# Causal attention: GpSimd zeroes the diagonal block's future probabilities in place of a triangle matmul on the scores

## The reference, cut to what matters

```python
scores = jnp.einsum('bqhd,bkhd->bhqk', q, k) * hd ** (-0.5)
causal = jnp.tril(jnp.ones((S, S), bool))
scores = jnp.where(causal, scores, jnp.finfo(scores.dtype).min)
attn = jax.nn.softmax(scores, axis=-1)
o = jnp.einsum('bhqk,bkhd->bqhd', attn, v).reshape(B, S, D)
```

## Time and profile before

| | |
|---|---|
| median of 3 runs | 2627.32 us (2627.03 to 2632.26) |
| the profiled execution | 2615.49 us, of which 2613.7 us from the first to the last instruction |
| busy over the span | TensorE 81%, VectorE 58%, ScalarE 41%, GpSimd 11% |
| mean granted clock of TensorE | 0.90 |
| causal attention | about 903 to 1385 us of the span |

### The profile page before, as it was taken

The page is one execution under the profiler, slowest core; times in us unless marked ns, Lnnn a source line. Parts: engine busy times, 40 slices in busy tenths (PEclk is TensorE's granted clock), DMA queues, the critical chain, the costliest instruction groups (busy, mean ns, idle before and its releaser), DMA issues. The chain is left out here.

```text
span 2613.7 us, 46760 instructions
## 1 busy us (share of the span) xinstructions
PE 2105.6 (81%) x14586; PEld 1292.0 (49%) x14587; DVE 1521.3 (58%) x3119; ACT 1076.9 (41%) x1974; POOL 294.3 (11%) x348
## 2 busy tenths in 40 slices
PE   7748999999599549999995850199999964899987
PEld 4402333333355325555554640188888852555654
DVE  5746777776166436666653864344444435677763
ACT  3415666666122115555551112233333323465552
POOL 1000000000111000000000006500000013312100
PEclk9968999999699769999997765599999987999999
DMA  6742333320357534444414538411111132111100
GB/s 204 261 122 70 85 97 86 93 74 22 117 161 241 178 112 112 118 131 120 130 61 148 174 110 286 156 49 45 49 49 48 45 100 65 53 61 41 56 9 17
DMA packets 212155, 271.53 MB, mean 104 GB/s; under 512 B 24929, under 2 KB 161018, under 8 KB 212018
## 3 DMA queue, kind: packets, MB, share of 16 engines
q1 hardware_dynamic: 205250, 252.70, 31.8%
q0 software_dynamic: 6144, 16.79, 1.9%
q10 hardware_dynamic: 624, 0.30, 0.1%
HBM read 159.77 MB, written 108.86 MB: 103 GB/s over the span
## 5 line engine op out<-in xcount | busy, mean ns | idle before, releaser
L749 ACT ACTIVATE a_prob<-a_psE 128x512 f32<-128x512 f32 (+3 forms) x1024 | 500.3, 519 | 508.5 <-PE a_psE L646 254.5
L630 PE MATMUL a_psS<-a_K,a_Q 97*128 97x512 bf16 (+3 forms) x1024 | 360.9, 358 | 117.7 <-DMA a_Q<-a_nrow 45.5
L782 DVE TENSOR_REDUCE a_nm<-a_psS 128x2 f32<-128x1024 f32 x256 | 312.9, 1225 | 136.6 <-PE a_psS L630 135.6
L643 PE MATMUL a_psE<-a_Q,a_K 100*128 100x512 bf16 (+3 forms) x1024 | 356.8, 351 | 37.9 <-DMA a_Q<-a_nrow 26.4
L779 DVE TENSOR_REDUCE a_nm<-a_psS 128x1 f32<-128x128 f32 (+3 forms) x512 | 238.3, 487 | 175.8 <-PE a_psS L633 173.6
L643 PEld LDWEIGHTS a_psE<-a_Q,a_K 100*128 100x128 bf16 x1024 | 103.2, 101 | 274.0 <-ACT a_prob L749 192.4
L1407 PE MATMUL ex_psH<-ex_xT,ex_w1h 128*128 128x256 f16 x1872 | 232.7, 275 | 3.6 <-ACT ex_xT L1366 2.1
L656 PE MATMUL a_psO<-a_prob,a_V 128*32 128x512 f32 (+3 forms) x2048 | 233.7, 529 | 1.4 <-ACT a_prob L749 1.4
L1421 PE MATMUL ex_psY<-ex_w2h,ex_hl 128*128 x1872 | 229.4, 272 | 0.5 <-DVEq L1332 0.4
L1375 ACT ACTIVATE ex_hf<-ex_psH,ex_b 128x256 f32<-128x256 f32 x312 | 131.2, 472 | 233.8 <-PE ex_psH L1407 233.8
L630 PEld LDWEIGHTS a_psS<-a_K,a_Q 97*128 97x128 bf16 x1024 | 103.5, 102 | 242.7 <-DVE a_nm L779 74.3
(11 more groups left out here) (253 smaller groups left out, 3154.6 us busy)
## 6 DMA issues: line engine op xcount, KB each, us to landing
s_qk<-t_parts SPq DMA_DIRECT2D x64, 384.0 KB, 3.2
s_v<-t_vaug SPq DMA_DIRECT2D x16, 1024.0 KB, 6.5
a_V<-s_v SPq DMA_DIRECT2D x64, 256.0 KB
s_o<-a_on SPq DMA_DIRECT2D x64, 256.0 KB, 2.1
t_cin<-s_o SPq DMA_DIRECT2D x16, 1024.0 KB, 8.4
ex_stage<-in_w SPq DMA_DIRECT2D x16, 1024.0 KB, 6.7
a_K<-s_qk SPq DMA_DIRECT2D x64, 192.0 KB
a_Q<-s_qk SPq DMA_DIRECT2D x64, 192.0 KB
```

The costliest lines, as they stand in the source:

```text
L630: last = pe.matmul(bank[:, 0:n], Q6[s][0:K_MAX, h, t * P:(t + 1) * P], K6[s][0:K_MAX, h, 0:n], start=True, stop=not causal)
L643: last = pe.matmul(bank[:, 0:S - q0], K6[s][0:K_EXP, h, t * P:(t + 1) * P], Q6[s][0:K_EXP, h, q0:S], start=True, stop=not causal)
L749: act.activation(prob[j % NP_BUF][:, 0:n], psE[j % NE][:, 0:n], ACT.Exp).then_inc(p_ready, 1)
L782: dve.tensor_reduce(nm[s % NM_BUF][:, t - 1:t + 1, h], psS_all[:, (j - 1) % NS:j % NS + 1, :], axis=AX.X, op=ALU.max, negate=True).then_in ...
```

## The change

The triangle `cmk` and its matmul in `shifted` go away. The exponential is then taken of unmasked scores on the diagonal block too. Behind each exponential GpSimd overwrites the future places of the first 128 columns of the `prob` tile by 0, with a select on position (`affine_select`), in place. `weigh` waits for the new semaphore `masked` in place of `p_ready`. The triangle `cmq` for the maxima stays. In the phase `a0` `masked` is `p_ready` itself and nothing changes.

GpSimd's loop now has 16 selects a step, and `rcx` of group G - 1 stands between the selects of units 10 and 11.

```diff
-    cmk = c.sb("cmk", [P, P], BF16)
+    masked, seen = (c.sem("masked"), c.sem("seen")) if causal else (p_ready, None)
...
+            def widen(n, s):
+                pool.wait_ge(rc_ready, n)
+                pool.tensor_tensor(rcx[s][:].rearrange("p (h m) -> p h m", m=HP),
+                                   rc[s][:].unsqueeze(2).to_broadcast([P, TT * GH, HP]),
+                                   one[:].to_broadcast([P, TT * GH, HP]), ALU.mult).then_inc(rcx_ready, 1)
+
+            def future_out(G, j):
+
+                pool.wait_ge(p_ready, G * U + j + 1)
+                pool.sem_inc(seen, 1)
+                square = prob[j % NP_BUF][:, 0:P]
+                pool.affine_select(out=square, in_=square, compare_op=ALU.is_ge, fill=0.0, base=0,
+                                   pattern=[[1, P]], channel_multiplier=-1).then_inc(masked, 1)
+
+            def step(G, s):
+                for j in range(U):
+                    future_out(G, j)
+                    if j == 10 and not (isinstance(G, int) and G == 0):
+                        widen(G, (s - 1) % 2)
+
+            if causal:
+                steps(pool, step)
+                widen(G_ALL, (G_ALL - 1) % 2)
+                return
...
-                last = pe.matmul(bank[:, 0:S - q0], K6[s][0:K_EXP, h, t * P:(t + 1) * P], Q6[s][0:K_EXP, h, q0:S],
-                                 start=True, stop=not causal)
-                if causal:
-                    last = pe.matmul(bank[:, 0:P], identb[:], cmk[:], start=False, stop=True)
-                last.then_inc(e_ps, 1)
+                pe.matmul(bank[:, 0:S - q0], K6[s][0:K_EXP, h, t * P:(t + 1) * P], Q6[s][0:K_EXP, h, q0:S],
+                          start=True, stop=True).then_inc(e_ps, 1)
...
-                pe.wait_ge(p_ready, G * U + (t + 1) * GH)
+                pe.wait_ge(masked, G * U + (t + 1) * GH)
```

More of the change, by code:

```diff
@@ L510, in last_of @@
         return isinstance(G, int) and G + k >= G_ALL
-    n_set = 10 if causal else 6
+    n_set = 8 if causal else 6
     with nc.Block() as block:
@@ L530, in _ @@
                 pool.memset(cmq[:], 0.0).then_inc(set_done, 1)
-                pool.memset(cmk[:], 0.0).then_inc(set_done, 1)
-                pool.wait_ge(set_done, 8)
+                pool.wait_ge(set_done, 7)
                 pool.affine_select(out=cmq[:], in_=cmq[:], compare_op=ALU.is_ge, fill=NEG, base=0,
                                    pattern=[[-1, P]], channel_multiplier=1).then_inc(set_done, 1)
-                pool.affine_select(out=cmk[:], in_=cmk[:], compare_op=ALU.is_ge, fill=NEG, base=0,
-                                   pattern=[[1, P]], channel_multiplier=-1).then_inc(set_done, 1)
             pool.memset(one[:], 1.0).then_inc(one_set, 1)
             pool.wait_ge(one_set, 1)
+            def widen(n, s):
[18 more added lines that the diff above has]
+                return
             with pool.Fori(0, G_ALL // 2) as i:
                 for s in range(2):
[L543 to L546, removed]
+                    widen(i * 2 + (s + 1), s)
         @block.sync
```

## The result

| | before, same chip | after |
|---|---|---|
| median | 2628.72 us (4 runs) | 2662.62 us (4 runs, 2660.63 to 2669.22) |
| ratio | | 1.0132, 95% interval 1.0109 to 1.0154 |
| the profiled execution | 2615.49 us | 2660.65 us, span 2658.9 |

The change makes the kernel 34 us slower (29 to 40 by the interval); 14 were forecast. I compare the causal phase alone, from GpSimd's clearing of `cmq` at its start to the end of the last `scale`: 482.0 us before, 513.4 us after, +31.3.

What follows compares the result with a forecast made beforehand. TensorE was taken to bound the phase, with DMA waits at about half the step boundaries. Loaded steps +10, unloaded +3, last two +2.3, long waits -3, clock +2: about +14 on 2627.3, so 2641 us; range 2620 to 2663.

Steps and rivals of the forecast that it cites:

- The mechanism: `rcx` queued behind unit 10's select on GpSimd makes TensorE stall 1.45 us before `spread` in every step.
- The select: Each 128x128 select on GpSimd takes 0.29 us; sixteen and an `rcx` fill 5.7 us of a 12 us step.
- The rival of a dear select: Selects dearer than 0.29 us or held up by VectorE: 0.5 us more a step by `rcx`, 2656 us; chance 0.06.
- TensorE's loop without loads: The step when TensorE's stream alone sets it, as in 4 steps: from 12.12 to 12.87 us.
- the `weigh` behind unit 5: First part of a step: waits for unit 3's exponential, then 0.43 us in place of 0.38; gain 0.13, not 0.35.
- Sum for the phase: Adds the causal phase's changes over first step, 25 steps with loads, 4 without and last two: about +14 us.
- long waits that go: Long DMA waits at step boundaries lose 3 us to the slack that the new stall gives.
- the DMA loop: Step start to `scale`, then the maxima's DMA to the step after next: from 12.6 to 13.0 us a step.
- The last two: +2.3: Last two steps, without `score`: longer stall before `spread`, triangles still go; +1.1 us each and 0.1 at the end.
- The clock rival: The clock falls behind every stall before `spread`: TensorE's step 14.07 us in 29 steps, +34, 2661 us; chance 0.10.
- The exchange: The stall before `spread` changes places with the boundary wait for the maxima's DMA: +2, 2629 us; chance 0.18.
- the faster rival: Every boundary wait goes, and the low clock behind long ones: -6 us in all, 2621 us; chance 0.14.

Runs made afterwards that it cites:

- the first experiment: The changed kernel with `rcx` moved from behind the select of unit 10 to behind that of unit 8: 2634.70 us, ratio 1.0018.

## Why the prediction was right in its mechanism and wrong in its size

- **The mechanism.** Right. `rcx` behind unit 10 stalls `spread` in every step. From unit 10's `shifted` to `spread` 2.16 us were worked out and 2.21 measured; TensorE would arrive there at 0.81, as the kernel with `rcx` behind unit 8 shows, and not at 0.70, so the stall is 1.40 us and not 1.45. Making it late without selects costs 22 us, bringing it forward gives back 29.
- **The select.** Right: 0.293 us for 0.29, GpSimd far from being a bound. The rival of a dear select fell with it. VectorE's L816, the one of its four short steps with two SBUF inputs that stands in the midst of selects, went from a median of 164 to 185 ns, with 277 the longest. Its price is at most the 8.1 us of waiting before `maxima` in 23 steps. The Trainium skill (SBUF — State Buffer, Who interferes with whom) speaks of an exclusive lock that blocks the other engine for a whole instruction, which could be up to 293 ns here; the trace shows a median of 21 ns more and 113 at most in 30 steps, less than a whole select.
- **TensorE's loop without loads.** Nearly: 12.87 forecast, 13.16 measured. The stall was right, the gain was not: without the stall I had 0.67 us a step of gain (0.44, and the 0.23 between unit 10 and `spread`), and the first experiment shows 0.41. Part of the rest is in the `weigh` behind unit 5: I had argued that it comes 0.05 us later after its exponential, and it comes 0.22 later (0.60 us for 0.38).
- **The failing step: "Sum for the phase".** For the 25 steps with loads I put +10, less 3 for long waits that go and 2 more for the clock, +9; they cost 18.5, and 16.7 with the loop written out. The sum took the DMA loop as the bound after the change as well (13.0 us, half of the delay passed on). But TensorE's own loop came out at 13.16, above it, and steps with loads then ran another 0.27 over it. Written out, where no halt blurs it, the step goes from 12.68 us, close to the 12.6 of the DMA loop, to 13.40 and not to 13.0. The experiment one place later confirms it: a lengthening of 0.39 in the stall passed on as 0.35. What keeps a loaded step above TensorE's own loop (13.10 to 12.12 before, 12.69 to 11.72 with `rcx` behind unit 8) shrinks as that loop grows, but doesn't go to nothing, and I had let it. The 18.5 can be read in another way too: with the loop the 21 ordinary steps cost 6.8, no more than their share of the +9, and 11.7 stand in the four around the branches, of which 6.8 are the longer halts (13.1 us of waiting in place of 6.4). That term I had at nothing. The runs don't settle how much is due to each reading, since without the loop the loss is in the ordinary steps.
- **"The last two: +2.3".** They cost 9.8. I had priced the stall and forgotten that these are the steps with the least work around it: the clock fell behind it and stayed at 0.50 for the phase's last 27 us. With the stall taken from these two steps alone 8.7 us come back.
- **The clock rival, 2661 us.** Its number is 2 us from the result, and its mechanism is wrong: the clock stayed at 1.00 behind the stalls of the dense steps. A right total is no evidence for the sum behind it.
- **The exchange and the faster rival.** The boundary waits did shrink, 12.0 to 3.0 us, as both said. This exchange gives back 9 us of some 43, not all.
- **Not forecast.** The second halt at the branch. It makes the table of steps hard to read. With `rcx` behind unit 8 it costs 11 us; its part in after was not measured by itself, and the whole change costs 27 to 31 us without the loop, where there is no halt, against 34 with it.

## What to carry to other kernels

On an in-order queue the place of an instruction is a dependency. When a quiet engine is given work that another one paces, find what already stood on its queue and who waits for that, and put the urgent instruction ahead of the paced ones: here two places were worth 29 us, and the exchange of triangles for selects by itself 1 to 6. Before taking matmuls off the busiest engine, run the kernel with them simply left out, and look at what else that moves: here it gave nothing with the loop, as the second halt came with it, and 9 to 12 us with the loop written out. Price a stall separately where the work around it is thin, since the clock can fall there.

## What the runs showed of the hardware that I had not expected

- A branch back over a long loop body (eight steps here) holds TensorE's sequencer for 3.3 to 4.1 us, and once for 5.05, against 0.06 us on VectorE and 0.05 us on ScalarE and GpSimd at the same branches. In every looped kernel here whose TensorE stream lacks the triangle 2.8 to 4.4 us more follow, which 32 idle instructions ahead of the loop took away. Written out, the kernel before gains 0.6%.
- A stall of 1.4 us in each of 29 dense steps of 13 us left the granted clock at 1.00; one in a step without `score` was followed by 0.50 for the remaining 27 us of the phase.
